# A graph network's front: one program ahead of the first edge pass, and the rest of the preparation beside it

## The chip, the cores and the metric

One core of one Trainium2 chip. The metric is the device time of one execution in microseconds; the kernel before was run three times. The profile is one execution of the same program, taken by the hardware profiler.

## What is computed

The inputs are 3125 nodes with 256 features, 50000 edges (src, dst, sorted by dst, and a weight), and the weights of four graph blocks. Each block is added to its input, and a layer norm follows:

```python
x = _layernorm(x + L0(x, src, dst, edge_weight, ...))   # 3 layers: linear, / sqrt(deg_out), per-channel product,
                                                        # weighted sum over the edges of a node, / sqrt(deg_in), relu
x = _layernorm(x + L1(x, src, dst, ...))                # max over edges of relu(theta(x_dst - x_src) + phi(x_src))
x = _layernorm(x + L2(x, edge_index, ...))              # attention with 8 heads, softmax over the edges of a node
x = _layernorm(x + L3(x, src, dst, ...))                # 3 layers: max over the edges of a *source*, batch norm, relu
```

So the kernel needs, beside the features: how many edges each node has as a source and as a target (deg_out, deg_in), where each node's edges begin and end in both orders, and for block L3 the order of the edges by source.

## The kernel before, in words

**Tiles.** 128 edges make a tile, 4 tiles a group: 392 tiles, 98 groups (`NG`). The nodes are 25 tiles. A program is a chain of stages (`Stage`), each with its own semaphores; every engine ends one stage before the next begins.

**Ahead of the first edge pass** (lines 261 to 716) come five stages, and then the node products n0:
- `constants`: identity, triangular masks, iotas.
- `edge_columns`: src, dst and weight are loaded, turned by TensorE and stored as columns; zeros are written to DRAM.
- `histogram(0)` counts by dst, with all weight loads beside it on SP. A node number is split into 98 high and 32 low digits. For 14 tiles at a time VectorE makes two one-hots (line 521, called from 550 and 551), TensorE multiplies them tile by tile (573), ScalarE copies the 98x32 counts of each tile to `HIST` (588). After 28 such steps VectorE adds `HIST` over the tiles (553) and forms starts by running sums (555 to 560), which go to DRAM.
- `histogram(1)` does the same by src. Beside it: the node numbers of dst (616 to 645), 25 indirect writes of marks by GpSimd (650), the weight transposes (387) and weight products (394, 400).
- `src_nodes`: 32 running sums over `HIST` (703), the numbers of src, and roots.
- `node_products("n0")`: per node tile a copy (1065), a transpose (993), a product (1000), ScalarE's scaled copy (1081) and VectorE's end (1086); each fifth tile SP stores five tiles of the table (1050). GpSimd writes the 25 marks of src.

**Edge passes** (`edge_pass`, 1096): e0, e1, e2 belong to the three layers of L0, e3 to L1, and others follow. Per group g: SP prefetches indices, mask and weights six groups ahead (1117 to 1120); GpSimd gathers four tiles (1146) into one of six sets; ScalarE scales them (1208, `scale`); TensorE turns them ("forth", 1161); VectorE runs a segmented scan in two halves (1191, `scan`); TensorE turns them back ("hither", 1170); ScalarE copies them (1215, `evac`); SP stores them. `pipelined` writes the order of each engine: every step has a lead, and step (fn, lead) does group s+lead in iteration s, in the order in which the steps are listed, "early" ones ahead of the pass's own and "late" ones behind.

**Rank work beside them** (`rank_beside`, 735): for each edge its place in the order by src. For one group of four tiles (a rank step k): one-hots on VectorE (521), "flip" on TensorE (787, 788), "take" on ScalarE (808 to 810), "meet" on TensorE (796 to 798), "places" on VectorE (769 to 776). "flip" k waits for "places" k-1, "places" k for "meet" k. Each of e0, e1 and e2 does a third of the steps, one every three groups. `order_beside` in e3 turns the ranks into the order.

Of the kernel before, what the change touches and what calls it, by code (L numbers as in the profile page):

```python
# [72 lines left out]
def pipelined(total, unroll, eng, *steps):  # L84

    most = max(lead for _, lead in steps)
    turns = (total - max(most, 3)) // unroll
# [8 lines left out]
    with eng.Fori(0, turns) as i:  # L98
        for j in range(unroll):
            for fn, lead in steps:  # L100
                fn(i * unroll + (j + lead), (j + lead) % unroll, i + (j + lead) // unroll)
    for s in range(turns * unroll, total):
        straight(s)
# [54 lines left out]
def build(nc, a, out):  # L158
    top = ExitStack()
    Stage.used = []  # L160
    with top:
# [7 lines left out]
        def carve(base, *wanted):  # L169
# [38 lines left out]
        HIST, key_hi, key_lo = carve(ARENA[:, NT * RW:NT * 3 * RW], ((ET, LO), F32), ((ET,), F32), ((ET,), F32))  # L208

        oh_hi, oh_lo, = carve(AGW_BASE, ((2, HB, HI), BF16), ((2, HB, LO), BF16))  # L210
        rank_hi, rank_lo, rank_t, rank_tf, rank_tmp, sel, rank = carve(
            AGW_BASE, ((2, RB, HI), BF16), ((2, RB, LO), BF16), ((2, 2, RB * P), BF16), ((2, RB * P), F32),
# [4 lines left out]
        key_tmp, iota_i, SRCF = carve(WORK, ((3, ET), I32), ((ET,), I32), ((ET,), F32))  # L217
# [12 lines left out]
        MW = sb("MW", [P, LAYERS, 2, D])  # L230
        TH1, DF1, W2 = sb("TH1", [P, 2, D]), sb("DF1", [P, 2, D]), sb("W2", [P, 2, D])
        WA = sb("WA", [P, 2, 2 * HEADS])
        TH3, DF3 = sb("TH3", [P, LAYERS, 2, D]), sb("DF3", [P, LAYERS, 2, D])
# [10 lines left out]
        MV = sb("MV", [P, NT, 2])  # L244
# [12 lines left out]
        flag_dst, flag_src = dram("flag_dst", [EP, 1]), dram("flag_src", [EP, 1])  # L257
        hist_start, hist_count = dram("hist_start", [2, NP]), dram("hist_count", [2, NP])


        def constants():
            with Stage(nc, "cst") as st:
                zeroed, filled, done = st.sem("zeroed"), st.sem("filled"), st.sem("done")
                copied = st.sem("copied")
                block = st.block()

                @block.gpsimd
                def _(eng):
                    eng.memset(ident[:, :], 0.0).then_inc(zeroed, 1)
                    eng.memset(ones[:, :], 1.0).then_inc(zeroed, 1)  # L270
                    eng.iota(iota_i[:, :], pattern=[[1, ET]], base=0, channel_multiplier=0).then_inc(zeroed, 1)
                    eng.wait_ge(zeroed, 3)
# [5 lines left out]
                    eng.affine_select(out=upto[:, :], in_=ones[:, :], compare_op=ALU.is_ge, fill=0.0,  # L278
                                      base=0, pattern=[[1, P]], channel_multiplier=-1).then_inc(filled, 1)

                @block.vector
                def _(eng):
                    eng.wait_ge(filled, 3)
                    eng.tensor_copy(identb[:, :], ident[:, :]).then_inc(copied, 1)
                    eng.tensor_copy(iota_b[:, :], iota_i[:, 0:P]).then_inc(copied, 1)
                    eng.tensor_copy(iota_h[:, :], iota_i[:, :]).then_inc(copied, 1)


        def weights_beside():


            fc, ch, mlp, th1, ph1, w2, fcb, fcb_wide, prod, AV = carve(
                WORK[:, 5 * ET:WORK.shape[1]], ((LAYERS * 2, D), F32), ((LAYERS * 2, D), F32), ((2, LAYERS * D), F32),
                ((2, D), F32), ((2, D), F32), ((2, D), F32), ((LAYERS * 2,), F32), ((LAYERS * 2, P), F32),
                ((2, 2, D), F32), ((2, D), F32))
            th3, ph3, B1b = carve(AGW_BASE[:, HB * (HI + LO):NT * RW], ((LAYERS * 2, D), F32), ((LAYERS * 2, D), F32), ((D,), F32))

            turns = [(lambda m, k, l=l: mlp[:, m, l * D + k * P:l * D + k * P + P], MW[:, l]) for l in range(LAYERS)]
            turns += [(lambda m, k: th1[:, m, k * P:k * P + P], TH1[:, :, :]),
                      (lambda m, k: ph1[:, m, k * P:k * P + P], DF1[:, :, :]),  # L300
                      (lambda m, k: w2[:, m, k * P:k * P + P], W2[:, :, :])]
            turns += [(lambda m, k, l=l: th3[:, 2 * l + m, k * P:k * P + P], TH3[:, l]) for l in range(LAYERS)]
            turns += [(lambda m, k, l=l: ph3[:, 2 * l + m, k * P:k * P + P], DF3[:, l]) for l in range(LAYERS)]
            banks = len(turns) + 2 * LAYERS

            def load_stage(st):
                loaded, zeroed = st.sem("loaded"), st.sem("zeroed")

                def on_sync(eng):
                    n = 0  # L310

                    def load(dst, src):
                        nonlocal n
                        eng.dma_start(dst, src).then_inc(loaded, 16)
                        n += 16

                    load(X[:, 0:NT - 1, :], a["x"][0:(NT - 1) * P, :].rearrange("(t p) d -> p t d", p=P))
                    eng.wait_ge(zeroed, 2)
                    load(X[0:LAST, NT - 1, :], a["x"][(NT - 1) * P:N, :])
                    load(fc, a["L0_gnn_fc_w"].rearrange("l (k p) i -> p (l k) i", p=P))  # L320
                    for c in range(4):
                        for l in range(LAYERS):
                            load(ch[64 * (c % 2):64 * (c % 2) + 64, 2 * l + c // 2, 64 * c:64 * c + 64],
                                 a["L0_gnn_ch_w"][l, c])
                    load(mlp, a["L0_gnn_mlp_w"].rearrange("(m p) i -> p m i", p=P))
                    with nc.allow_non_contiguous_dma("a bias across the partitions"):
                        load(fcb, a["L0_gnn_fc_b"].rearrange("l (k p) -> p (l k)", p=P))
                    for dst, name in ((th1, "L1_gnn_theta_w"), (ph1, "L1_gnn_phi_w"), (w2, "L2_gnn_W")):
                        load(dst, a[name].rearrange("(m p) i -> p m i", p=P))
                    for dst, name in ((th3, "L3_gnn_thetas"), (ph3, "L3_gnn_phis")):  # L330
                        load(dst, a[name].rearrange("l (m p) i -> p (l m) i", p=P))

                    def spread(dst, src, width):
                        load(dst, src.broadcast_to([P, width]))

                    spread(CHB[:, :, :].rearrange("p l d -> p (l d)"),
                           a["L0_gnn_ch_b"].rearrange("(o l) c d -> o (l c d)", o=1), LAYERS * D)
                    spread(MB[:, :], a["L0_gnn_mlp_b"].rearrange("(o d) -> o d", o=1), D)
                    spread(B1[:, :], a["L1_gnn_theta_b"].rearrange("(o d) -> o d", o=1), D)
                    spread(B1b, a["L1_gnn_phi_b"].rearrange("(o d) -> o d", o=1), D)  # L340
                    spread(AV[:, 0, :], a["L2_gnn_a_left"].rearrange("(o h) c -> o (h c)", o=1), D)
                    spread(AV[:, 1, :], a["L2_gnn_a_right"].rearrange("(o h) c -> o (h c)", o=1), D)
                    spread(GAM[:, :, :].rearrange("p l d -> p (l d)"),
                           a["L3_gnn_gammas"].rearrange("(o l) d -> o (l d)", o=1), LAYERS * D)
                    spread(BET[:, :, :].rearrange("p l d -> p (l d)"),
                           a["L3_gnn_betas"].rearrange("(o l) d -> o (l d)", o=1), LAYERS * D)
                    eng.wait_ge(loaded, n)

                def on_gpsimd(eng):
                    eng.memset(X[:, NT - 1, :], 0.0).then_inc(zeroed, 1)  # L350
                    eng.memset(ch, 0.0).then_inc(zeroed, 1)

                return dict(sync=on_sync, gpsimd=on_gpsimd)
# [1532 lines left out]
```

## Time and profile before

| what | us |
|---|---|
| median of three runs | 5416.98 |
| lowest, highest | 5415.43, 5417.36 |
| the profiled execution: span from first to last instruction (no other time of it is shown) | 5421.3 |
| busy in it: TensorE matmuls | 3436.3 |
| busy in it: VectorE | 3334.7 |
| busy in it: GpSimd | 3323.9 |
| busy in it: ScalarE | 1890.6 |

All times in rows are microseconds from the start of the span, unless marked ns. PE is TensorE's matmuls, PEld its weight loads, DVE VectorE, ACT ScalarE, POOL GpSimd, SP the engine that issues the other DMAs. "PEclk" is the granted clock of TensorE as a share of its full 2.4 GHz. L521 is line 521 of the kernel. The number in brackets at a row's end is the idle time of the engine in front of it, and what ended it. A line such as L521 belongs to a helper and stands for the calls in both counts and in the rank work.

### The profile page before, as it was taken

The page shows a single profiled execution, that of the slowest core. Times are in us where ns is not written, and L with a number is a line of the kernel's source. Part 1 is how long each engine was busy: PE and PEld are TensorE (multiplying, and loading weights), DVE is VectorE, ACT ScalarE, POOL GpSimd, SP SyncE. Part 2 cuts the span into 40 slices and gives each one's busy share as a digit, 9 for nine tenths or more (in the row PEclk, how much of TensorE's full clock was granted, in tenths as well). Part 3 has the DMA queues.
Part 4 walks back from the last instruction along what each step waited for, and adds up shares of the span by engine and source line. Part 5 has one row for each costly group of instructions (what it writes and reads, how often), then busy time and mean ns, then how long its engine had stood idle before and what let it go on. Part 6 is the DMA issues. An engine that isn't in the chain of part 4 may idle for free. (4 is left out here: it accounts for less than half of the span.)

```text
span 5421.3 us, 80197 instructions
## 1 busy us (share of the span) xinstructions
PE 3436.3 (63%) x18554; PEld 2760.3 (51%) x18554; DVE 3334.7 (62%) x6781; ACT 1890.6 (35%) x4275; POOL 3323.9 (61%) x3460
## 2 busy tenths in 40 slices
PE   3577777777787866666646664455556555665552
PEld 3456665666566655444534442355545555455451
DVE  8856655666566657999657775644444444444444
ACT  2256654666366643222223332222212222122221
POOL 1367765777477744777456664277752777357771
PEclk9778778788877778999666776777778777677776
DMA  3078875888488844888369995288853888358881
GB/s 89 16 197 235 235 210 151 239 234 234 128 236 234 235 136 137 234 233 234 110 170 241 248 242 152 65 230 236 237 163 103 236 237 236 96 169 235 236 230 52
DMA packets 965249, 1026.24 MB, mean 189 GB/s; under 512 B 312526, under 2 KB 843784, under 8 KB 965168
## 3 DMA queue, kind: packets, MB, share of 16 engines
q1 hardware_dynamic: 801184, 582.41, 36.8%
q0 software_dynamic: 163984, 442.92, 31.3%
q8 instruction: 30, 0.49, 0.0%
q14 instruction: 51, 0.42, 0.0%
HBM read 573.30 MB, written 449.41 MB: 189 GB/s over the span
## 5 line engine op out<-in xcount | busy, mean ns | idle before, releaser
L1146 POOL DMA_INDIRECT WORK<-table,idxbuf x2744 | 2609.6, 951 | 1319.6 <-issue 763.8
L1191 DVE TENSOR_TENSOR_SCAN WORK<-maskbuf,WORK,e_fm 128x512 f32<-128x512 bf16 x1372 | 1681.1, 1267 | 1293.7 <-PE e_fm L1161 1287.4
L1161 PE MATMUL e_fm<-ident,WORK 128*128 128x128 f32 x5488 | 997.2, 340 | 1044.1 <-DMA WORK<-table,idxbuf 717.5
L1161 PEld LDWEIGHTS e_fm<-ident,WORK 128*128 128x128 f32 x5488 | 790.1, 175 | 1218.8 <-DMA WORK<-table,idxbuf 725.2
L1215 ACT ACTIVATE WORK<-e_em 128x512 f32<-128x512 f32 x1372 | 757.1, 588 | 1607.6 <-PE e_em L1170 1491.3
L1170 PE MATMUL e_em<-ident,WORK 128*128 128x128 f32 x5488 | 995.2, 342 | 109.4 <-DVE WORK L1191 109.3
L1170 PEld LDWEIGHTS e_em<-ident,WORK 128*128 128x128 f32 x5488 | 884.6, 184 | 134.7 <-issue 112.4
L1208 ACT ACTIVATE WORK<-WORK,wbuf 128x256 f32<-128x256 f32 x1176 | 501.0, 496 | 605.2 <-DMA WORK<-table,idxbuf 605.2
L1545 POOL DMA_INDIRECT WORK<-table_attention,idxbuf x392 | 378.2, 965 | 189.5 <-issue 109.2
L1575 PE MATMUL att_o<-WORK 128*128 128x264 f32 x784 | 297.1, 543 | 0.0
L993 PE MATMUL n_t<-ident,WORK 128*128 128x128 f32 x450 | 108.9, 329 | 264.2 <-DVE WORK L966 156.3
L993 PEld LDWEIGHTS n_t<-ident,WORK 128*128 128x128 f32 x450 | 52.2, 156 | 339.0 <-DVE WORK L966 164.3
L1575 PEld LDWEIGHTS att_o<-WORK 128*128 128x128 f32 x784 | 199.5, 267 | 47.9
L521 DVE TENSOR_TENSOR ARENA<-ARENA,iota_b 128x128 bf16<-128x128 bf16 (+5 forms) x308 | 187.2, 665 | 1.4 <-DVEq L758 0.7
L1662 ACT ACTIVATE WORK<-att_o 128x264 f32<-128x264 f32 x392 | 151.1, 389 | 78.2 <-PE att_o L1575 73.4
L1559 PE MATMUL att_a<-ident,ARENA 128*32 128x128 f32 x98 | 33.4, 341 | 220.7 <-ACT ARENA L1649 220.1
L798 PE MATMUL e_ra<-ARENA 98*128 (+1 forms) x784 | 171.2, 302 | 0.0
L1329 PE MATMUL bn_ps<-ARENA,ones 128*128 128x256 f32 x300 | 105.0, 522 | 89.0 <-DVE ARENA L1355 79.0
L1559 PEld LDWEIGHTS att_a<-ident,ARENA 128*32 128x32 f32 x98 | 9.7, 99 | 274.9 <-ACT ARENA L1649 273.5
L798 PEld LDWEIGHTS e_ra<-ARENA 98*128 98x128 f32 x784 | 126.5, 203 | 28.8
L1329 PEld LDWEIGHTS bn_ps<-ARENA,ones 128*128 128x128 f32 x300 | 77.4, 266 | 116.6 <-DVE ARENA L1355 87.2
L844 DVE TENSOR_SCALAR ARENA<-iota_b,ARENA 128x128 bf16<-128x128 bf16 x392 | 133.3, 340 | 0.0
(282 smaller groups left out, 4519.9 us busy)
## 6 DMA issues: line engine op xcount, KB each, us to landing
edge_results<-WORK SPq DMA_DIRECT2D x686, 512.0 KB
edge_results_attention<-WORK SPq DMA_DIRECT2D x98, 544.0 KB
WORK<-table,idxbuf POOLq DMA_INDIRECT x2744
maskbuf<-nst_dst SPq DMA_DIRECT2D x294, 128.0 KB
maskbuf<-low_src SPq DMA_DIRECT2D x294, 128.0 KB, 4.9
ARENA<-dst_row SPq DMA_DIRECT2D x98, 256.0 KB
table<-ARENA SPq DMA_DIRECT2D x35, 640.0 KB, 3.2
maskbuf<-low_dst SPq DMA_DIRECT2D x98, 128.0 KB
```

Source lines behind the costliest of these rows:

```text
L521: return eng.tensor_tensor(dst, key[:, ds(t, n)].unsqueeze(2).broadcast_to([P, n, width]), iota_b[:, 0:width].unsqueeze(1).broadcast_to([P ...
L798: last = eng.matmul(pa[:, n * LO:(n + 1) * LO], rank_tf[0:HI, b, cols], HIST[0:HI, ds((k + first) * RB + n, 1), :].rearrange("p o l -> p ( ...
L993: last = eng.transpose(tp[slot][:, k * P:(k + 1) * P], R[:, slot, k * P:(k + 1) * P], ident[:, :])
L1146: eng.indirect_dma_start(G[:, q * GT + k, 0:D], None, T, bass.IndirectOffsetOnAxis(ap=idxbuf[:, q, k:k + 1], axis=0)).then_inc(got[q].sem, 16)
L1161: last = eng.transpose(fm[:, q % 2, h, k * P:(k + 1) * P], G[:, q * GT + k, h * P:(h + 1) * P], ident[:, :])
L1170: last = eng.transpose(em[:, pair, k, h * P:(h + 1) * P], S[:, q % 2, h, (2 * pair + k) * P:(2 * pair + k + 1) * P], ident[:, :])
L1191: last = eng.tensor_tensor_scan(S[:, q % 2, h, :], maskbuf[:, q, :], fm[:, q % 2, h, :], S[:, 1 - q % 2, h, GT * P - 1:GT * P], op0, op1)
L1208: last = eng.activation(G[:, q * GT + k, 0:D], G[:, q * GT + k, 0:D], ACT.Copy, scale=wbuf[:, q, k:k + 1])
L1215: eng.activation(O[:, q % 2, 2 * pair:2 * pair + 2, 0:D], em[:, pair], ACT.Copy).then_inc(pairs, 1)
L1329: last = eng.matmul(dst, ones[0:n, :], src[0:n, t, :], start=t == 0, stop=t == NT - 1)
L1545: eng.indirect_dma_start(G[:, q * GT + k, :], None, T2, bass.IndirectOffsetOnAxis(ap=idxbuf[:, q, k:k + 1], axis=0)).then_inc(got[q].sem, 16)
L1575: eng.matmul(po[:, k, 0:TW], same[:, q % 2, k, :], G[:, q * GT + k, :], start=True, stop=True).then_inc(made, 1)
```

## The change

- The stages from `constants` to n0 become one stage, `setup`. It loads src first, counts by src alone (28 steps, in two halves of 14, with the turning of dst and weight and the layer weight products of L0 between them), lets GpSimd add up `HIST` step by step, picks the counts of the nodes with one matmul, and makes the first table from X, whose turning reads X itself. The masks come from comparing each edge's dst with the edge before it; the marks of dst are gone.
- `e0` is written out flat (no loop) and carries in place of ranks: the count by dst (8 tiles a group, summed in PSUM), the node numbers of src and dst, the other weight loads and transposes, and the 32 running sums over `HIST`, one to a group.
- The ranks are done in e1 and e2, one step every two groups, with other leads and three buffers.
- The 25 marks of src move from n0 to n4. The keys of the one-hots become bf16.

```diff
-        HIST, key_hi, key_lo = carve(ARENA[:, NT * RW:NT * 3 * RW], ((ET, LO), F32), ((ET,), F32), ((ET,), F32))
+        HIST, key_hi, key_lo, dkey_hi, dkey_lo, node_f = carve(
+            ARENA[:, NT * RW:NT * 3 * RW], ((ET, LO), F32), *[((ET,), BF16)] * 4, ((6, NT), F32))
...
+                    eng.memset(added[0:HI], 0.0).then_inc(summed, 1)
+                    with eng.Fori(0, steps) as i:
+                        eng.wait_ge(held, i + 3)
+                        eng.wait_ge(summed, i + 1)
+                        eng.tensor_tensor(added[0:HI], added[0:HI], HIST[0:HI, ds(i * HB, HB), :], ALU.add).then_inc(summed, 1)
...
+                    split(SRCI[:, :], key_hi, key_lo)
...
+                    hots(0, half // 2)
+                    eng.wait_ge(gcn_in, 14 * 16)
+                    for q in range(2 * LAYERS):
+                        eng.tensor_scalar(fcb_wide[:, q, :], ones[:, :], fcb[:, q:q + 1], None, ALU.mult).then_inc(wide, 1)
+                    hots(half // 2 * 2, (steps - half // 2 * 2) // 2)
...
+                    eng.wait_ge(summed, steps + 1)
+                    c.link(eng.tensor_reduce(count_src[:, :], added[0:HI].rearrange("p t l -> p l t"), AX.X, ALU.add))
+                    c.link(spread_counts(c, count_src, spread[0:HI, :].rearrange("p (q l) -> p q l", q=4)))
+                    eng.sem_inc(spread_sem, 1)
+                    eng.wait_ge(picked, 1)
+                    c.link(eng.tensor_scalar(norm_out[:, :], picked_ps[:, 0:NT], 1.0, None, ALU.max))
...
+                def extras(g, q, turn):
+                    if g < groups:
+                        if g >= 2:
+                            eng.wait_ge(dmade, g - 1)
+                        one_hot(eng, dhi[:, g % 2], dkey_hi, g * DB, DB, HI).then_inc(dhot, 1)
+                        one_hot(eng, dlo[:, g % 2], dkey_lo, g * DB, DB, LO).then_inc(dhot, 1)
...
+                    if groups + 9 <= g < groups + 9 + LO:
+                        lo = g - (groups + 9)
                         c.inc(eng.tensor_tensor_scan(HIST[0:HI, :, lo], ones[0:HI, 0:1].broadcast_to([HI, ET]),
+                                                     HIST[0:HI, :, lo], start_src[:, lo:lo + 1], ALU.mult, ALU.add))
...
-        RANKS = -(-(ET // RB) // LAYERS)
+        RANKS = ET // RB // 2
-            first = layer * RANKS
-            steps = min(RANKS, ET // RB - first)
+            first = (layer - 1) * RANKS
+            steps = RANKS
...
-                        if q % 3 == phase and not (isinstance(g, int) and g // 3 >= steps):
-                            fn(turn * (SETS // 3) + q // 3, q // 3 % 2)
+                        if q % 2 == phase and not (isinstance(g, int) and g // 2 >= steps):
+                            fn(turn * (SETS // 2) + q // 2, q // 2)
...
-                    return [(at(0, meet), 0)], [(at(0, flip), 2)]
+                    return [], [(at(0, meet), 0), (at(0, flip), 1)]
...
-                    return [(at(0, take), 1)], []
+                    return [(at(0, take), 0)], []
...
-            node_products("n0", stage_copy(X), GW[:, 0], out1, None, out2, table=(AGG, T), marks=(first_src, flag_src))
             for l in range(LAYERS):
-                edge_pass(f"e{l}", SRCI, (ALU.mult, ALU.add), nst_dst, True, rank_beside(l))
+                edge_pass(f"e{l}", SRCI, (ALU.mult, ALU.add), nst_dst, True, rank_beside(l) if l else numbers_and_weights_beside)
...
-            node_products("n4", None, DF1, copy_to(AGG), TH1, out2, table=(AGG, T), norm=(add_bias,))
+            node_products("n4", None, DF1, copy_to(AGG), TH1, out2, table=(AGG, T), norm=(add_bias,), marks=(first_src, flag_src))
...
-        constants()
-        edge_columns()
-        load_weights, turn_weights = weights_beside()
-        histogram(0, DSTF, load_weights)
-        histogram(1, SRCF, both_beside(turn_weights, dst_nodes_beside))
-        src_nodes()
+        setup()
         flow_l0()
```

VectorE's steps of the rank work keep their leads: "places" early with lead 0 in odd groups, one-hots late with lead 3.

## Rows read from the trace of the kernel before

**Rows 1.** Windows: length, PE, PEld, DVE, ACT, POOL busy (count), PEclk, DMA share, GB/s
```profile
242.20:291.60 49.40, 37.33 (x158) 24.80 (x158) 18.70 (x53) 20.52 (x50) 24.48 (x25) 0.88 0.24 71
291.60:800.30 508.70, 390.48 (x2352) 326.80 (x2352) 313.77 (x623) 309.09 (x687) 374.39 (x392) 0.79 0.83 228
870.90:1380.00 509.10, 388.33 (x2360) 323.94 (x2360) 314.62 (x626) 308.13 (x686) 373.45 (x392) 0.79 0.81 227
...
2034.00:2090.00 56.00, 45.90 (x214) 34.74 (x213) 40.65 (x152) 29.45 (x81) 0.00 (x0) 1.00 0.14 50
```

**Rows 2.** Groups of instructions in e0 (291 to 785): busy and mean ns, idle before
```profile
L1146 POOL DMA_INDIRECT WORK<-table,idxbuf x392 | 374.4, 955 | 136.1 <-issue 106.0 <-DMA wbuf<-WE 30.1
```

**Rows 3.** Timeline (start, us): n0's last tile, e0's first and last gather
```profile
282.47 0.48 DVE L1086 SCALAR_TENSOR_TENSOR ARENA<-GB,norm_out,WORK 128x256 f32<-128x256 f32 x1 [0.38 <-ACT WORK L1081]
...
291.62 0.99 POOL L1146 DMA_INDIRECT WORK<-table,idxbuf  x1 [17.00 <-DMA wbuf<-WE]
...
784.19 0.94 POOL L1146 DMA_INDIRECT WORK<-table,idxbuf  x1 [0.30 <-issue]
```

**Rows 4.** Ahead of the first pass: groups by form, and the first count's timeline row
```profile
L521 DVE TENSOR_TENSOR ARENA<-ARENA,iota_b 128x1372 bf16<-128x1372 bf16 x56 | 88.6, 1583 | 0.7 <-DVE ARENA L512 0.7
L650 POOL DMA_INDIRECT flag_dst<-ones,first_dst x25 | 43.1, 1725 | 105.3 <-DVEq L673 97.9 <-issue 7.3
L553 DVE TENSOR_REDUCE count<-ARENA 98x32 f32<-98x12544 f32 x2 | 42.8, 21376 | 4.4 <-ACT ARENA L588 4.4
L521 DVE TENSOR_TENSOR ARENA<-ARENA,iota_b 128x448 bf16<-128x448 bf16 x56 | 34.8, 621 | 0.0
...
L703 DVE TENSOR_TENSOR_SCAN ARENA<-ones,startv,ARENA 98x392 f32<-98x392 f32 x32 | 29.7, 1009 | 5.2 <-PEq L155 5.2
...
20.13 57.02 DVE L521 TENSOR_TENSOR ARENA<-ARENA,iota_b 128x1372 bf16<-128x1372 bf16 x56 [0.35 <-DVE ARENA L512]
```

**Rows 5.** Timeline: the weight products of L0, the first and the last of them
```profile
183.64 1.89 PE L394 MATMUL w_ps<-WORK 128*128 128x256 f32 x8
...
191.62 0.38 ACT L416 ACTIVATE GB<-w_ps 128x256 f32<-128x256 f32 x1 [0.27 <-PE w_ps L400]
```

**Rows 6.** Timeline of TensorE in e2 at full clock: flip, forth (then hither), meet's first and last
```profile
1512.62 0.22 PE L787 MATMUL e_ra<-identb,ARENA 128*98 128x128 bf16 x1
...
1513.97 1.09 PE L1161 MATMUL e_fm<-ident,WORK 128*128 128x128 f32 x8
...
1515.77 0.22 PE L796 MATMUL e_rb<-ARENA 98*128 98x128 bf16 x1
...
1517.74 0.41 PE L798 MATMUL e_ra<-ARENA 98*128 x2
```

**Rows 7.** Timeline of ScalarE in e0: the first of take's three copies
```profile
784.73 0.58 ACT L808 ACTIVATE ARENA<-e_ra 98x512 bf16<-98x512 bf16 x1
```

**Rows 8.** Timeline of VectorE in e0: places, its first and last, and the scans
```profile
788.90 0.29 DVE L769 SCALAR_TENSOR_TENSOR ARENA<-e_rb,upto 128x128 bf16<-128x128 f32 x1 [1.40 <-PE e_ra L798]
...
790.39 0.16 DVE L776 TENSOR_TENSOR BYSRC<-ARENA 128x4 f32<-128x4 f32 x1
...
791.92 2.45 DVE L1191 TENSOR_TENSOR_SCAN WORK<-maskbuf,WORK,e_fm 128x512 f32<-128x512 bf16 x2 [1.37 <-PE e_fm L1161]
```

**Rows 9.** Timeline of TensorE in e2 at half clock: meet's first, then forth, hither
```profile
1531.18 0.31 PE L796 MATMUL e_rb<-ARENA 98*128 98x128 bf16 x1
...
1534.74 1.95 PE L1161 MATMUL e_fm<-ident,WORK 128*128 128x128 f32 x8
1536.48 1.91 PE L1170 MATMUL e_em<-ident,WORK 128*128 128x128 f32 x8
```

**Rows 10.** Windows (columns as in rows 1): a gap of TensorE in e2, and behind it
```profile
1549.90:1553.20 3.30, 0.38 (x4) 0.14 (x2) 2.61 (x3) 1.68 (x5) 2.43 (x3) 0.96 0.85 258
1553.20:1556.50 3.30, 3.22 (x16) 3.22 (x17) 1.03 (x1) 0.99 (x3) 2.65 (x3) 0.52 0.73 223
1556.50:1562.80 6.30, 5.18 (x40) 3.86 (x37) 4.23 (x5) 5.70 (x13) 4.78 (x6) 1.00 0.82 248
```

More of the change, by code:

```diff
@@ L97, in pipelined @@
         straight(s)
[L98 to L101, printed above, removed]
+    if turns:
+        with eng.Fori(0, turns) as i:
+            for j in range(unroll):
+                for fn, lead in steps:
+                    fn(i * unroll + (j + lead), (j + lead) % unroll, i + (j + lead) // unroll)
     for s in range(turns * unroll, total):
@@ new lines, in build, with one_hot @@
+        count_dst, start_dst, small = (v[0:HI] for v in carve(ROWSUMS, ((LO,), F32), ((LO,), F32), ((LO + 2,), F32)))
+        pick, rows_of = sb("pick", [HI, NT]), sb("rows_of", [HI, 4])
+        START, CNT, HAS, LASTE, T1, T2_ = range(6)
+        def one_hot(eng, dst, key, t, n, width):
+            return eng.tensor_tensor(dst, key[:, ds(t, n)].unsqueeze(2).broadcast_to([P, n, width]),
+                                     iota_b[:, 0:width].unsqueeze(1).broadcast_to([P, n, width]), ALU.is_equal)
@@ new lines, in _, with hots @@
+                    split(SRCI[:, :], key_hi, key_lo)
+                    def hots(first, turns):
+                        with eng.Fori(0, turns) as i:
+                            for b in range(2):
+                                n = i * 2 + (first + b)
+                                eng.wait_ge(made, n + 1)
+                                one_hot(eng, oh_hi[:, b], key_hi, n * HB, HB, HI).then_inc(hot_sem, 1)
+                                one_hot(eng, oh_lo[:, b], key_lo, n * HB, HB, LO).then_inc(hot_sem, 1)
@@ L602, in histogram @@
-            if which == 1:
-                gathered[0].close(NT)
-        node_f, flag_cols, mark_cols = carve(AGW_BASE[:, HB * (HI + LO) + (4 * LAYERS + 1) * D:NT * RW], ((6, NT), F32), ((ET,), F32), ((3, ET), BF16))
-        START, CNT, HAS, LASTE, T1, T2_ = range(6)
-        def load_numbers(eng, w, loaded):
-            with nc.allow_non_contiguous_dma("node numbers across the partitions"):
-                for k, h in ((START, hist_start), (CNT, hist_count)):
-                    eng.dma_start(node_f[:, k, :], h[w:w + 1, :].rearrange("o (t p) -> p (o t)", p=P)).then_inc(loaded, 16)
+                    eng.wait_ge(dst_in, 48)
@@ new lines, in _, with hold @@
+                    eng.activation(rows_f[:, 1], rows_i[:, 1], ACT.Copy).then_inc(cast_dst, 1)
+                    eng.sem_inc(held, 2)
+                    def hold(first, turns):
+                        with eng.Fori(0, turns) as i:
+                            for b in range(2):
+                                n = i * 2 + (first + b)
+                                eng.wait_ge(made, n + 3)
+                                eng.activation(HIST[0:HI, ds(n * HB, HB), :],
+                                               wide_ps[0:HI, b, 0:HB * LO].rearrange("p (k l) -> p k l", l=LO), ACT.Copy).then_inc(held, 1)
```

796 lines of the change are left out of this document (417 added, 379 removed).

## The prediction

> **What bounds the kernel now.** I read the stage table first. It cuts the run at the block borders: everything ahead of the first edge pass takes 291.6 us, of which the last 49.4 us are the first node products; then the edge passes e0 and e1 take 508.7 and 509.1 us each, with node products between them [rows 1]. The reader is to see two kinds of time. In an edge pass GpSimd holds the pace: 392 indirect gathers of 0.955 us busy, with 0.30 us of issue between two, so one every 1.25 us and 5.0 us for a group of four tiles; the last gather starts 492.6 us after the first, which is 391 times 1.26 [rows 2, 3]. In e1 VectorE is busy 315 of 509 us and TensorE 388, at a mean granted clock of 0.79 of full speed [rows 1]: both have room, but the rank work rides on that room. Ahead of the first pass, VectorE is the bound, with two counts in a row: 56 pairs of one-hots (1583 and 621 ns, a pair every 2.04 us, since 56 instructions take 57.0 us), two reductions of 21.4 us, and 32 running sums of 1.01 us [rows 4].
>
> **The part in front.** The change puts one program there. Its path, term by term:
> - Start of the count: today at 20.1 us [rows 4], behind three blocks and all nine edge loads. Now only src is awaited. I take 9 us, between 5 and 20.
> - 28 pairs for src alone: 57.0 us [rows 4], so 66.
> - TensorE leaves the count in the middle to turn two columns and to form the layer weights. The weight products took 8.0 us, 183.6 to 191.6 [rows 5], the turns perhaps 1.5; VectorE has six small products (1.3) and two one-hot pairs (4.1) in hand and waits for the rest. I add 7.5 us in all: 73.5.
> - Last matmuls, last copy and GpSimd's last addition: 3.5 us, so 77. GpSimd's addition of 98x448 has no row. Nothing, if it hides; if it takes 3 us where a step has 2.04, 28 steps cost 27 us more. I take it as hidden, nearest to VectorE's pair, which covers four times as many elements in 2.04 us.
> - The short reduction, the spreading, one matmul, root and reciprocal: 5 us, 82.
> - First node products without the copy ahead of each turn: they took 40.7 us (242.2 to 282.9) [rows 1, 3]; I take 36, so 118. Between its last tile and the first gather lay 8.7 us [rows 3], kept: first gather at 127.
>
> So the first gather moves from 291.6 to 127: **-165 us**, between -130 and -178. Gone are the second count's 57 us, both 21.4 us reductions, and the 32 sums from the path.
>
> **Work moved into e0.** Per group, VectorE's scans take 2.45 us [rows 8] and the new one-hots (1040 elements, against 1820 in 2.04 us [rows 4]) 1.2: 3.7 of 5.0 us. TensorE gets 8 small matmuls and, every second group, four turns. In return e0 loses its third of the ranks. The node numbers are bursts of a few us, and six sets of gathered tiles lie ahead. The weight loads, some 3.5 MB behind SP's prefetches, would be 15 us at the 228 GB/s of the pass [rows 1], and SP issues eight of them between the prefetches of groups 1 to 3. The 32 running sums come one to a group from group 58 on, 1.0 us in 2.5 free. I take **+3 us**, between 0 and +15; if the gathers' cover is gone, the prefetch is late next. The 25 marks for src go from n0 to n4, where GpSimd is idle for 56 us [rows 1]; at the dearest rate seen, 1.73+0.30 us each [rows 4], they need 51, and stand ahead of e3's gathers in GpSimd's queue. Nothing, and up to +5. The longer straight code of e0: nothing, bounded by the same +15.
>
> **The ranks, now in two passes instead of three.** This is what I think decides. The rank step runs every two groups (10.0 us of gathers) instead of every three (15.0), and its leads are shorter: TensorE's "meet" now stands behind hither(2k), and VectorE's "places" in front of scan(2k+1). Until now a whole iteration lay between them. Now they form a ring:
> - scan(2k) ends; hither(2k) 0.9; meet(k) 2.2 and its tail 0.3 (1515.8 to 1518.15) [rows 6]; places(k) 1.65 [rows 8]; scan(2k+1) 2.45 [rows 8];
> - then on VectorE one-hots 0.8 and scan(2k+2) 2.45, which closes the ring: 0.9+2.5+1.65+2.45+0.8+2.45 = 10.75, with waits some 10.85 us. On TensorE in the same time: hither 0.9, flip 1.35, forth 0.9, hither 0.9, meet 2.5 [rows 6] after the 4.1 of places and scan: 10.65. ScalarE's "take", three copies of 0.6 us that overlap to 1.5 [rows 7], fits beside forth and hither.
>
> So at full clock the ring already needs 10.85 us where gathers need 10.0. At half clock meet takes 3.55 and forth or hither 1.74 [rows 9]; flip I take as 1.8: 4.1+1.74+1.8+1.74+1.74+3.9 with waits is 15.4 us. TensorE stands still in each round from the end of forth(2k+2) to the end of scan(2k+1), about 3.5 us. The windows show what follows such a gap: after 3.3 us with 0.38 of work the clock of the next 3.3 us was 0.52, that is 1.2 GHz, and full (2.4 GHz) again behind it [rows 10]. If each round pays one such stretch, 3.3 us at half speed do 1.65 us of work and the round is 10.85+1.65 = **12.5 us**. A pass has 49 rounds: 49 x (12.5-10.0) = +122 us each, **+245** for e1 and e2, between 0 (the ring slips under the gathers after all) and +530 (15.4). What is queued behind: VectorE waits for "meet" with its scans behind it; TensorE's hither, ScalarE's copies, SP's stores and the next prefetches follow.
>
> **Sum.** The profiled execution shows its span alone, 5421.3 us, 4.3 above the median of 5417.0. 5421.3 - 165 + 3 + 245 = 5504; less 4.3: **5500 us**.
>
> **Rivals.**
> 1. Ring at full clock. TensorE has more work per us than before, which speaks for it; three passes at 0.79 [rows 1] speak against. Round 10.85: +42 per pass, 5339 us. Point of decision: the saved 162 us are 81 per pass, a round of 11.65 us. Below it the kernel is faster.
> 2. The gathers keep the pace, as in every pass now; e1 and e2 stay at 509: 5255. It needs an overlap that I don't see in the order of the code.
> 3. Half clock throughout: 15.4 a round, 5785. Against it: the clock came back in e1 each time.
> 4. GpSimd's addition paces the count (3 us a step): +27, 5527.
> 5. One-hots at twice the rate, since the keys are now bf16: 57 us become about 30, 5473. Against it: with f32 keys or bf16 keys there is no pair of rows to compare; today's pair runs at 1.1 ns an element [rows 4].
> 6. The program in front doesn't overlap as it says and the first gather comes at 200, 73 us later than I have it: 5573.
>
> On rival 5 the Trainium skill says both: "VectorE: DVE Perf Modes" gives the doubled rate to a two-source operation whose tensors are all 16-bit with step one; "Vector Engine (DVE) Microarchitecture Reference" (5.1, the triggers) adds that one element read again and again, as the key is here, ran at the single rate. By the first the sum would be 27 us less, by the second it stands.
>
> **How the numbers follow.** Forecast 0.48; rival 1 0.21; 2 0.13; 3 0.05; 4 0.04; 5 0.05; 6 0.04. A change under 0.2% (11 us) is about what a measurement of this kernel can't tell from none. Faster: rivals 1 and 2 and a tail of the forecast, 0.37; same 0.04; slower 0.59. The forecast's own range, rounds of 11.8 to 14.1 us, is 5430 to 5660. The range 5320 to 5650 takes in rival 1 with the bounds of the part in front and leaves out rivals 2 and 3, 0.18.
>
> **What would show it.** First gather near 127 us (the part in front). L521's mean in the count still about 1.58 us (rival 5). e0 still near 509 us. In e1 and e2: GpSimd's gathers wait for prefetched indices instead of issue, 392 gathers over some 600 us; VectorE's "places" group has a large idle time in front, released by TensorE's L798 line, near 3.4 us a round; granted clock 0.75 to 0.85. I am wrong in size if that clock is 1.0, and wrong in kind if gathers still follow each other every 1.25 us there, or if e0 or the marks in n4 have grown.

## Result, and the profile after

The changed kernel takes **5644.0 us** (median of 4, 5641.2 to 5658.6), the kernel before 5417.1 in the same comparison: a ratio of **1.0425**, 95% interval 1.041 to 1.044. So it is slower, as forecast, but by 227 us and not by 83, and it lies inside the given range by 6 us only. The profiled execution has a span of 5641.5 us; its ledger against the 5421.3 of before adds up to the difference of the two spans, 220 us. (The 227 us are those of the medians: the median lies 2.5 us above the profiled span here and lay 4.3 below it before.)

| stretch | before | after | difference | forecast |
|---|---|---|---|---|
| first gather of e0 | 291.6 | 139.9 | -151.7 | -165 |
| e0, first to last gather | 492.6 | 517.6 | +25.0 | +3 |
| e0's last gather to e1's first | 91.9 | 90.3 | -1.6 | 0 |
| e1, first to last gather | 491.6 | 650.8 | +159.2 | +122 |
| to e2's first gather | 91.1 | 108.6 | +17.5 | 0 |
| e2, first to last gather | 492.5 | 653.1 | +160.6 | +122 |
| to e3's first gather (n3, n4 and the marks) | 145.5 | 160.7 | +15.2 | 0 |
| all behind that | 3324.5 | 3320.5 | -4.0 | 0 |

The stages by windows, for [rows 1] (length, PE, PEld, DVE, ACT and POOL busy with their counts, PEclk, DMA share, GB/s): the part in front, e0, e1, e2, and e2's last tail with n3 and n4.

```profile
0.00:139.90 139.90, 78.57 (x592) 68.73 (x592) 100.92 (x112) 41.51 (x90) 48.21 (x53) 0.83 0.27 86
139.90:663.00 523.10, 309.08 (x1997) 287.58 (x1997) 341.08 (x384) 265.47 (x596) 393.72 (x392) 0.74 0.83 226
...
747.70:1420.00 672.30, 492.18 (x2723) 396.59 (x2723) 340.76 (x816) 336.18 (x733) 373.74 (x392) 0.74 0.62 171
...
1507.00:2182.00 675.00, 496.06 (x2729) 399.86 (x2729) 340.61 (x816) 336.60 (x733) 374.51 (x392) 0.74 0.61 170
2182.00:2320.90 138.90, 92.48 (x418) 67.40 (x417) 89.99 (x300) 55.33 (x152) 50.07 (x50) 0.88 0.18 57
```

In e1 GpSimd does the 373.7 us of work that it did before, over 672 us, and what the transfers move falls from 227 to 171 GB/s: neither sets the pace. In e0 the transfers keep 226 GB/s, but GpSimd is busy 393.7 us instead of 374.4 for the same 392 gathers.

**Who waits in e1.** The view of one line: the gathers of e1, then the first step of "places" there (count, shortest, median and longest duration in ns, first and last start; below it what its engine waited for).

```profile
L1198 POOL DMA_INDIRECT WORK<-table,idxbuf x392: 940/946/1304, 747.7 to 1398.6; - x196
its engine sat idle before it (us, times) until:
  DMA wbuf<-WE: 212.2, 53
  issue: 107.5, 339
...
L819 DVE SCALAR_TENSOR_TENSOR ARENA<-e_rb,upto x196: 284/286/293, 766.8 to 1422.7; 128x128 bf16<-128x128 f32 x196
...
  PE e_ra L848: 309.6, 49
```

The gathers wait for prefetched indices (212 us in 53 waits), and VectorE stands 309.6 us in 49 waits ahead of places, released by the last line of meet: 6.3 us a round. That is the forecast's signature with the wrong size, 3.4 us. From the first places to the first instruction of the last (1422.02 on the timeline) are 48 rounds in 655.2 us: **13.65 us a round**, where I had 12.5.

**One round**, on the timeline of e1 (start, length in us; a row can hold several instructions in a row):

```profile
1053.74 0.29 DVE L819 SCALAR_TENSOR_TENSOR ARENA<-e_rb,upto 128x128 bf16<-128x128 f32 x1 [6.35 <-PE e_ra L848]
...
1055.69 2.45 DVE L1243 TENSOR_TENSOR_SCAN WORK<-maskbuf,WORK,e_fm 128x512 f32<-128x512 bf16 x2 [0.17 <-issue]
...
1058.06 0.74 DVE L255 TENSOR_TENSOR ARENA<-ARENA,iota_b 128x392 bf16<-128x392 bf16 x2
...
1058.29 1.96 PE L1222 MATMUL e_em<-ident,WORK 128*128 128x128 f32 x8 [3.67 <-DVE WORK L1243]
1058.72 2.44 DVE L1243 TENSOR_TENSOR_SCAN WORK<-maskbuf,WORK,e_fm 128x512 f32<-128x512 bf16 x2
...
1060.04 0.31 PE L837 MATMUL e_ra<-identb,ARENA 128*98 128x128 bf16 x1
...
1061.99 1.97 PE L1213 MATMUL e_fm<-ident,WORK 128*128 128x128 f32 x8
...
1063.75 1.47 PE L1222 MATMUL e_em<-ident,WORK 128*128 128x128 f32 x8
...
1065.05 0.22 PE L846 MATMUL e_rb<-ARENA 98*128 98x128 bf16 x1
```

The order is the one that was read out of the code: places, scan(2k+1), then on TensorE hither (1058.3), flip (1060.0), forth (1062.0), hither (1063.8) and meet (1065.1), which releases the next places. TensorE stands 3.67 us for the scan, and comes back slowly: hither takes 1.96 us and forth 1.97, where forth took 1.09 at full clock [rows 6]. Windows over the same round, columns as above (the eleventh number is the granted clock):

```profile
1053.40:1058.20 4.80, 1.21 (x10) 0.98 (x10) 4.10 (x14) 0.60 (x2) 3.30 (x4) 0.96 0.64 195
1058.20:1064.00 5.80, 5.71 (x26) 4.65 (x27) 2.96 (x4) 3.10 (x7) 4.27 (x5) 0.50 0.60 180
1064.00:1067.60 3.60, 3.60 (x27) 2.94 (x26) 0.14 (x1) 3.60 (x10) 0.00 (x0) 0.91 0.66 126
```

Behind a window with 1.21 us of work in 4.8 the clock is 0.50 (1.2 GHz). It stays there for 5.8 us in which TensorE is busy 5.71, and for 0.6 us more: a window of 1064.0 to 1064.6 has 0.50 too, and one from there to 1067.6 has 1.00 (2.4 GHz). So TensorE does 6.3 us of its work slowly, from the start of hither until just before meet. From round to round this repeats: behind the first, the 47 rounds of e1 are all between 13.50 and 13.72 us long.

**The part in front.** Groups of VectorE and of GpSimd up to the first gather, by form (count, busy us and mean ns, idle before), for [rows 4]:

```profile
L255 DVE TENSOR_TENSOR WORK<-ARENA,iota_b 128x1372 bf16<-128x1372 bf16 x28 | 59.8, 2135 | 7.8 <-PE set_wide L417 7.4 <-DVE ARENA L486 0.4
L255 DVE TENSOR_TENSOR WORK<-ARENA,iota_b 128x448 bf16<-128x448 bf16 x28 | 20.2, 723 | 0.0
...
L334 POOL TENSOR_TENSOR WORK<-WORK,ARENA 98x448 f32<-98x448 f32 x28 | 39.9, 1424 | 49.3 <-ACT ARENA L552 48.7 <-POOL WORK L334 0.6
```

And the timeline: the start of the count, its short reduction, the last tile of the node products, the first gather, and four gathers of e0.

```profile
9.77 14.88 DVE L255 TENSOR_TENSOR WORK<-ARENA,iota_b 128x1372 bf16<-128x1372 bf16 x11 [0.35 <-DVE ARENA L486]
...
98.45 0.90 DVE L509 TENSOR_REDUCE count_src<-WORK 98x32 f32<-98x448 f32 x1 [3.05 <-POOL WORK L334]
...
130.89 0.48 DVE L528 SCALAR_TENSOR_TENSOR ARENA<-GB,norm_out,WORK 128x256 f32<-128x256 f32 x1 [0.60 <-ACT WORK L580]
...
139.88 1.11 POOL L1198 DMA_INDIRECT WORK<-table,idxbuf  x1 [41.53 <-DMA wbuf<-WE]
...
178.35 0.95 POOL L1198 DMA_INDIRECT WORK<-table,idxbuf  x1 [0.30 <-issue]
179.60 1.74 POOL L1198 DMA_INDIRECT WORK<-table,idxbuf  x1 [0.30 <-issue]
...
190.44 0.94 POOL L1198 DMA_INDIRECT WORK<-table,idxbuf  x1 [3.86 <-DMA wbuf<-WE]
...
197.40 0.94 POOL L1198 DMA_INDIRECT WORK<-table,idxbuf  x1 [2.09 <-DMA wbuf<-WE]
```

The same pair of one-hots that took 1583 and 621 ns before takes 2135 and 723 now: 18.3 us more over 28 pairs in busy time. GpSimd's addition is short, 1.42 us, and would fit beside a pair; but it doesn't run beside it for nothing. In e0 single gathers take up to 1.76 us instead of 0.945: 62 of the 392 rows of GpSimd's timeline are over 1.0 us (15 before), together 23 us over the rest, and VectorE is on a one-hot in 30.5 of those 81.7 us (of all 394 us of the gathers it is in 49). At 190.4 and 197.4 two gathers wait for prefetched indices: these are groups 9 and 10, whose prefetches are issued around the eight weight loads in SP's queue.

### The profile page after: what moved, and what is told of

The parts are those of the page before. It is cut to its first block and busy times, and to the rows that moved or that the text cites. A ratio compares the mean times of both kernels' runs of the same rounds, so it can differ in the third digit from the quotient of the medians.

```text
span 5641.5 us, 78233 instructions
## 1 busy us (share of the span) xinstructions
PE 3503.4 (62%) x18564; PEld 2828.2 (50%) x18564; DVE 3301.4 (59%) x6801; ACT 1869.6 (33%) x4237; POOL 3346.4 (59%) x3471
## 3 DMA queue, kind: packets, MB, share of 16 engines
q0 software_dynamic: 163184, 442.91, 30.5%
## 5 line engine op out<-in xcount | busy, mean ns | idle before, releaser
L1213 PE MATMUL e_fm<-ident,WORK 128*128 128x128 f32 x5488 | 1022.3, 347 | 1074.7 <-DMA WORK<-table,idxbuf 816.1
L1267 ACT ACTIVATE WORK<-e_em 128x512 f32<-128x512 f32 x1372 | 769.0, 590 | 2143.4 <-PE e_em L1222 2086.4
L1213 PEld LDWEIGHTS e_fm<-ident,WORK 128*128 128x128 f32 x5488 | 817.9, 180 | 1235.2 <-DMA WORK<-table,idxbuf 805.9
L1222 PE MATMUL e_em<-ident,WORK 128*128 128x128 f32 x5488 | 1054.9, 357 | 365.9 <-DVE WORK L1243 361.5
L1222 PEld LDWEIGHTS e_em<-ident,WORK 128*128 128x128 f32 x5488 | 933.9, 193 | 401.7 <-issue 357.8
L1595 POOL DMA_INDIRECT WORK<-table_attention,idxbuf x392 | 380.8, 971 | 186.9 <-issue 108.6
L819 DVE SCALAR_TENSOR_TENSOR ARENA<-e_rb,upto 128x128 bf16<-128x128 f32 x392 | 90.5, 287 | 622.1 <-PE e_ra L848 622.1
L1042 PE MATMUL n_t<-ident,WORK 128*128 128x128 f32 x400 | 97.1, 329 | 216.3 <-DVE WORK L1015 153.3
L1049 PE MATMUL n_m<-TURNED,WORK 128*128 128x256 f32 x600 | 180.0, 429 | 0.0
L1053 PE MATMUL n_m<-TURNED,WORK 128*128 128x256 f32 x600 | 158.8, 388 | 0.0
L255 DVE TENSOR_TENSOR ARENA<-ARENA,iota_b 128x392 bf16<-128x392 bf16 (+3 forms) x294 | 135.9, 504 | 0.5 <-DVEq L808 0.5
```

The lines of the kernel that those rows point to most:

```text
L1049: last = eng.matmul(mps[:, slot, 0:D], XT[:, slot, k * P:(k + 1) * P], w1[:, k, :], start=k == 0, stop=k == 1)
L1053: last = eng.matmul(mps[:, slot, D:D + n2], XT[:, slot, k * P:(k + 1) * P], w2[:, k, :], start=k == 0, stop=k == 1)
L1213: last = eng.transpose(fm[:, q % 2, h, k * P:(k + 1) * P], G[:, q * GT + k, h * P:(h + 1) * P], ident[:, :])
L1222: last = eng.transpose(em[:, pair, k, h * P:(h + 1) * P], S[:, q % 2, h, (2 * pair + k) * P:(2 * pair + k + 1) * P], ident[:, :])
L1267: eng.activation(O[:, q % 2, 2 * pair:2 * pair + 2, 0:D], em[:, pair], ACT.Copy).then_inc(pairs, 1)
L1595: eng.indirect_dma_start(G[:, q * GT + k, :], None, T2, bass.IndirectOffsetOnAxis(ap=idxbuf[:, q, k:k + 1], axis=0)).then_inc(got[q].sem, 16)
```

## The experiments

Four questions: is it the order of the rank step; is it the clock; what lengthens the one-hots; what lengthens e0. The lines are those of the changed kernel unless said otherwise. One thing has to be known to read the numbers: in the jobs whose labels have no number, and in that of both_2, two_hots_in_e0_2 and before_leads_moved_2, the transfers were slower, and the kernel before took 7167 to 7182 us instead of 5417. Windows over e0 in leads_restored, whose e0 is the changed kernel's, untouched:

```profile
138.00:807.00 669.00, 323.45 (x1992) 282.97 (x1993) 336.58 (x383) 267.92 (x591) 397.88 (x392) 0.66 0.62 176
```

176 GB/s where 226 were moved before. So the passes of those jobs say little about the order on the engines. The same kernels have further labels with a number, and the same expectations where none is quoted. The part in front can be read in either kind of job: the first gather came at 138.6 us in leads_restored and at 139.8 in leads_restored_2.

**1. The leads of the rank step restored.**

```diff
-                    return [], [(at(0, meet), 0), (at(0, flip), 1)]
+                    return [(at(0, meet), 0)], [(at(0, flip), 2)]
...
-                    return [(at(0, take), 0)], []
+                    return [(at(0, take), 1)], []
```

> Only the leads of the rank step change: TensorE's meet goes back ahead of forth (early), flip back to lead 2, ScalarE's take back to lead 1; the step stays at every second group. Theory ring (the order closes scan, hither, meet, places, scan into one chain of 13.3 us a round): the chain is open again, VectorE has 7.9 us of work in a round of 10, TensorE some 7.5 at full clock; e1 and e2 fall from 650.8 and 653.1 us (first to last gather) to between 492 and 520, and the time to about 5290 us. Rival period (a rank step every two groups is too much work for the pass in any order): at half clock forth, hither, flip and meet need 13.8 us a round, so the passes stay above 620 us and the time above 5580.

> The same kernel as leads_restored, since in the first job every transfer was slower than in the traces shown (the kernel before took 7169 us there, and e0, which the edit doesn't touch, 666 us from first to last gather instead of 518). Where the transfers run as in the trace of the changed kernel (e0 near 518 us), theory ring says e1 and e2 fall to between 492 and 520 us and the time to about 5290 us; rival period says passes above 620 us and a time above 5580.

With slow transfers: 6926 us, ratio 0.970 (0.961 to 0.979). There the restored order gains nothing in the passes: e1 and e2 take 747 and 738 us from first to last gather, and 728 and 717 in the same job with the changed kernel's order (the kernel of run 5). With normal ones: **5304.2 us** (4 runs) against 5419.1, ratio **0.979** (0.977 to 0.981). Windows of e1, and the view by line of the gathers and of places in e1:

```profile
747.70:1245.00 497.30, 440.36 (x2707) 356.40 (x2706) 343.64 (x816) 327.82 (x725) 373.75 (x392) 0.81 0.85 230
```

```profile
L1198 POOL DMA_INDIRECT WORK<-table,idxbuf x392: 940/946/1346, 750.2 to 1242.2; - x196
...
L819 DVE SCALAR_TENSOR_TENSOR ARENA<-e_rb,upto x196: 284/286/294, 764.8 to 1247.1; 128x128 bf16<-128x128 f32 x196
...
  PE e_ra L848: 53.5, 46
```

492 us from first to last gather, as in the kernel before, and VectorE waits 53.5 us for meet instead of 309.6, with the same work in the same 49 rounds, at the same period. Two leads and one place in TensorE's order are worth 340 us (5644.0 against 5304.2); which of the three does it alone wasn't tried. The rival of the period falls.

**2. The clock kept up in the order of the change.** TensorE makes 24 transposes of the unit matrix in front of every second hither, inside its pause; they compute nothing that is used.

```diff
+                        if "filler" in side and q % 2 == 1:
+                            eng.wait_ge(pairs, g * 2 + 3)
+                            for _ in range(side["filler"]):
+                                eng.transpose(em[:, 0, 0, 0:P], ident[:, :], ident[:, :])
                         eng.wait_ge(scanned, g + 3)
```

> The order of the changed kernel is kept, but ahead of every second hither TensorE makes 24 extra transposes of the unit matrix into a bank that is free then (about 2.7 us at full clock), inside the 3.9 us in which it now waits for the scan. Theory ring plus clock (the pause drops the granted clock to 0.50 and hither, flip and forth then take twice as long): the clock of e1 and e2 rises from 0.74 to above 0.95, a round falls from 13.3 us to about 10.9, each pass to some 530 us, the time to about 5395 us. Rival ring alone (the chain would be as long at full clock, for instance by semaphore waits): the round stays within 0.5 us of 13.3 and the time near 5640 or above.

> The same kernel as filler, for the same reason. Theory ring plus clock: granted clock of e1 and e2 above 0.95, a round of about 10.9 us, some 530 us a pass, near 5395 us in all. Rival ring alone: a round within 0.5 us of 13.3, near 5640 us or above. A third outcome, which the first job hints at (clock 0.74 in e1, GpSimd waiting 330 us for indices): the extra matmuls lengthen TensorE's own chain and the clock is not kept either, passes above 650 us.

With slow transfers 7041 us, with e1 and e2 at 790 and 836 us from first to last gather, above the 728 and 717 without the extra transposes; why isn't known. With normal ones **5388.3 us** (one run), 256 below the changed kernel, though TensorE has more to do. Windows of e1, and places:

```profile
747.70:1270.00 522.30, 468.29 (x3715) 398.47 (x3716) 328.62 (x789) 318.37 (x703) 366.07 (x386) 0.98 0.79 214
```

```profile
L819 DVE SCALAR_TENSOR_TENSOR ARENA<-e_rb,upto x196: 284/286/293, 771.9 to 1293.8; 128x128 bf16<-128x128 f32 x196
...
  PE e_ra L848: 175.5, 49
```

At a clock of 0.98 a round takes (1293.8 - 0.7 - 771.9)/48 = **10.86 us** (0.7 us from the first to the fourth instruction of places). The chain alone was forecast at 10.85. So of the 3.65 us by which a round passes the 10.0 of the gathers, 0.86 are the chain and 2.8 the clock. The "third outcome" (passes above 650 us) came only with slow transfers.

**3. The same leads in the kernel before**, at a step every three groups in three passes (lines of the kernel before).

```diff
-                    return [(at(0, meet), 0)], [(at(0, flip), 2)]
+                    return [], [(at(0, meet), 0), (at(0, flip), 1)]
...
-                    return [(at(0, take), 1)], []
+                    return [(at(0, take), 0)], []
```

> The kernel before, with its rank step every three groups in three passes, but with the leads of the changed kernel (meet late, flip lead 1, take lead 0). Theory ring: the chain is about as long as in the changed kernel, 13.3 us a round plus one scan more, against 15.0 us of gathers; at 2.45 us and a hither more it comes to between 15 and 16.5, so e0 to e2 grow from 492 to somewhere between 492 and 540 us and the time is 5417 to 5550. If the order alone did the damage whatever the period, each pass would grow by 159 us as in the changed kernel, to some 5890.

With slow transfers 7206 and 7225 us, beside 7167 and 7182 for the kernel before. With normal ones **5424.1 us** (one run) beside 5418.0: no difference that one run can tell. Windows of e1, the gathers of e1, and the waits there:

```profile
870.90:1380.00 509.10, 385.64 (x2337) 326.37 (x2337) 310.83 (x615) 315.34 (x684) 374.20 (x392) 0.74 0.81 227
```

```profile
L1146 POOL DMA_INDIRECT WORK<-table,idxbuf x392: 945/949/1316, 879.7 to 1372.2; - x196
```

```profile
DVE ARENA L769 <- PE e_ra L798: 121.0, 32, 5.3
```

The chain is there: VectorE now waits 121.0 us for meet in e1 (3.8 us each; 17.7 us in the kernel before), and the clock falls from 0.79 to 0.74. But 15 us of gathers a round cover it, 492.5 us as before. Behind the last gather of e0 and of e1 some 3 and 4 us are added. So the order alone costs at most a few us, the period alone (run 1) nothing from first to last gather, and both together 340 us.

**4. The ranks left out**, in e1 and e2 both (the passes behind then read other rows of the same size).

```diff
-... rank_beside(l) if l else numbers_and_weights_beside)
+... nothing_beside if l else numbers_and_weights_beside)
```

> Leaves out the whole rank work in e1 and e2 (the order by src that it feeds is replaced by the node numbers of src, so e5 to e7 read other rows of the same size). Whatever the mechanism inside the rank work, the two passes go back to the pace of the gathers: 492 us from first to last gather each, some 335 us less in all, near 5305 us. If e1 and e2 stay above 520 us, something other than the ranks (code, prefetches, edge loads) slows them, and both the ring and the period fall.

It ran with slow transfers only (6753 us), so the forecast of 492 us a pass stays untested; run 1 had answered the question. There e1 took 646.5 us from first to last gather, no more than the 667 of that run's e0, while with the ranks and restored leads it was 747 in the same job. So where transfers are slow, the ranks aren't free in the better order either.

**5. The total of the count by TensorE** instead of GpSimd's addition.

```diff
-                    with eng.Fori(0, steps) as i:
-                        ...
-                        eng.tensor_tensor(added[0:HI], added[0:HI], HIST[0:HI, ds(i * HB, HB), :], ALU.add).then_inc(summed, 1)
...
+                                    last = eng.matmul(total, oh_hi[:, b, k, :], oh_lo[:, b, k, :], start=False, stop=False)
```

> Leaves GpSimd's addition of the count out of the part in front; TensorE makes a second small matmul for each tile that accumulates the total in a bank of its own. Theory contention (VectorE's one-hots were 2135 and 723 ns there, 1583 and 621 before, because GpSimd's two-input addition runs beside them): they go back to near 1583 and 621 ns, the first gather moves from 139.9 to about 118 us, and the time falls by some 21 us, to 5620. Rival layout (the one-hots are slower because their buffers or keys lie elsewhere): they stay above 2050 ns and the first gather within 3 us of 139.9. If TensorE's doubled matmuls pace the count instead, the one-hots are short but a step takes over 2.1 us.

With slow transfers, which the part in front doesn't feel (6899 us in all): groups of VectorE up to 120 us, by form, and the first gather on the timeline:

```profile
L255 DVE TENSOR_TENSOR WORK<-ARENA,iota_b 128x1372 bf16<-128x1372 bf16 x28 | 44.5, 1588 | 17.6 <-PE set_pick L416 17.3 <-DVE ARENA L487 0.4
L255 DVE TENSOR_TENSOR WORK<-ARENA,iota_b 128x448 bf16<-128x448 bf16 x28 | 17.3, 619 | 0.0
```

```profile
130.43 1.11 POOL L1199 DMA_INDIRECT WORK<-table,idxbuf  x1 [121.55 <-DMA wbuf<-WE]
```

The one-hots are back at 1588 and 619 ns, so it was the addition beside them and not their layout. But the first gather moves by 9.5 us and not 21: VectorE now waits 17.3 us for the doubled matmuls instead of 7.4 for the pause alone. I had put the pacing by TensorE last.

**6. One-hots in two of e0's 49 groups only**, with the leads restored.

```diff
-                        one_hot(eng, dhi[:, g % 2], dkey_hi, g * DB, DB, HI).then_inc(dhot, 1)
-                        one_hot(eng, dlo[:, g % 2], dkey_lo, g * DB, DB, LO).then_inc(dhot, 1)
+                        if g < 2:
+                            ...
+                        else:
+                            eng.sem_inc(dhot, 2)
```

> Leads restored, and in e0 the one-hots for the count of dst are made in the first two of 49 groups only; the other groups count those two over again (the node numbers of dst, and so all sums over incoming edges, are other ones of the same size). Theory contention (62 gathers of e0 took over 1.0 us, 23 us more than the rest's 0.945 us in all, and VectorE was on the one-hots in 30.5 of those 81.7 us): e0 falls from 519 us to about 502, with fewer than 25 long gathers. Rival transfers (the weights' 2.4 MB more and the instruction loads of the straight code stretch e0): e0 stays above 512 us. TensorE's small matmuls are kept, so they aren't told apart from the rest.

With slow transfers e0 didn't fall. It took 687.6 and 688.5 us, 21 and 22 more than in the runs both and both_2 of the same jobs (666.2 and 666.4), for a reason that stays open, though the gathers over 1.0 us fell from 60 to 19 and from 57 to 22. With normal ones (the run two_hots_in_e0_3), the view by line and three rows of the timeline:

```profile
L1201 POOL DMA_INDIRECT WORK<-table,idxbuf x392: 942/946/2440, 140.2 to 648.2; - x196
```

```profile
182.40 0.94 POOL L1201 DMA_INDIRECT WORK<-table,idxbuf  x1 [2.19 <-DMA wbuf<-WE]
...
189.89 0.94 POOL L1201 DMA_INDIRECT WORK<-table,idxbuf  x1 [2.79 <-DMA wbuf<-WE]
...
197.22 0.94 POOL L1201 DMA_INDIRECT WORK<-table,idxbuf  x1 [2.65 <-DMA wbuf<-WE]
```

e0 takes 508.0 us instead of 519.3 (run 1) and 518.8 (run 7): the one-hots cost **about 11 us**, between the 17 of one theory and the less than 7 of the other. It is one run, and e0 with all its one-hots was 517.6 in the changed kernel and 523.3 in run 2, so 10 to 15 us fit. The rest is read in the same trace. Gathers wait for indices at groups 8 to 11, four waits of 8.4 us in all where 0.3 each is usual, so some 7 us near the weight loads; and 23 gathers are still over 1.0 us, by 9.7 us in all, with VectorE on the running sums (L737 there) in 10.3 of their 31.4 us. Both links, to the weight loads and to the running sums, are read and not tested.

**7. Both edits, 1 and 5.**

> The two edits together: the leads of the rank step restored, and the count's total accumulated by TensorE in place of GpSimd's addition. Theory ring gives 5304 (leads restored alone); theory contention takes off what the first gather moved in the run total_on_pe, 139.9 to 130.4 us, so 9.5 us: about 5294 us, under the kernel before by some 2.3%. If the earlier first gather is given back in e0 or later, it stays at 5304.

> The same kernel as both. Where the transfers run as in the traces shown: 9.5 us under leads_restored_2, so about 5294 us, 2.3% under the kernel before; if the earlier start is given back, 5304.

With slow transfers 6896 and 6928 us, ratios 0.963 (0.959 to 0.966) and 0.966 (0.962 to 0.970). With normal ones **5286.1 us** (5 runs) against 5418.0, ratio **0.9756** (0.9742 to 0.9769), and the view by line for e0:

```profile
L1199 POOL DMA_INDIRECT WORK<-table,idxbuf x392: 943/949/2007, 129.2 to 648.1; - x196
```

The first gather is 10.6 us earlier than in run 1 (139.8) and the span 11.4 us shorter (5284.4 against 5295.8): what the part in front gains arrives at the end. The medians of the two lie 18 us apart instead (5286.1 and 5304.2); the four runs of run 1 spread over 15.5 us, so the difference to the 9.5 forecast isn't one that they can tell. This version beats both kernels.

## Why the forecast was right in kind and short in size

The forecast was +83 us, the measured change +227. The 144 us between them are: 13.3 in the part in front, 22 in e0, 107.5 in e1 and e2 with what stands behind their last gathers, -5.6 in the other stretches, and 6.8 because the median lies above the profiled span and not below it.

- **Direction and mechanism: right, and shown.** The order of the code closes a chain hither, meet, places, scan, one-hots, scan. Undoing the order alone brings 340 us back; its length at full clock is 10.86 us, forecast 10.85.
- **The clock term is the step that failed: right in kind, mis-sized, and some 107 of the 144 us that were missing.** "If each round pays one such stretch, 3.3 us at half speed do 1.65 us of work ..." The stretch is 6.3 us of work at 0.50, of which half is 3.15 us; by run 2 it costs 2.8 us a round. The round is 13.65 and not 12.5. I took the length of the slow stretch from one gap, where the next window was back at full clock [rows 10]. The rows that I used for the prices at half clock said otherwise: meet begins slow at 1531.18, and hither, at 1536.48, is slow still [rows 9], over 7 us. A short and a long stretch were both in hand, and I priced with the shorter one. That a round pays 6.3 us and not 3.3 or 7 is measured; why it is that long stays open. Per pass 49 x 3.65 = 179 us, measured 177 and 176.
- **Where it shows: half right.** I set the whole loss inside the passes. The gathers run up to six groups ahead, so 159 and 161 us stand between first and last gather, and 17.5 and 15.2 behind the last one, while the chain works off what is gathered. With the -1.6 us between e0 and e1 that is all of the growth from e0's end to e3. The marks in n4 cost nothing that can be seen, as forecast: in run 1, where the chain is open, e2's last gather to e3's first takes 145.3 us with the marks, and took 145.5 before.
- **The part in front: -151.7, forecast -165.** Start at 9.8 (9 forecast); end of the count at 95.0 (73.5); reduction to reciprocal 7.5 us (8.5); node products 28.9 us (36); to the first gather 8.5 (8.7). The term that failed is "I take it as hidden": the addition's length is hidden, its effect on the one-hots isn't. Rival 4 had the right place and nearly the price (+27), with the wrong mechanism: GpSimd doesn't pace the count, it waits 48.7 us in it for ScalarE's copies. Node products 7 us cheaper than forecast made up a third.
- **e0: +25, forecast +3** and at most +15. I asked what VectorE had room for (3.7 of 5.0 us) and what the transfers added, and not what VectorE's work does to GpSimd, which sets the pace. Of it about 11 us are the one-hots (shown, by one run); some 5 to 7 stand near the weight loads (I had named 15 and then taken 3), and the rest goes with the running sums, both as read in the traces.
- **The other rivals.** Rival 1 (ring at full clock) is what run 2 made, 5388 with the other terms as they are; rival 2 (gathers keep pace) is run 1. Rival 3 had the clock low throughout; it was 0.74. Rival 5 is out: with bf16 keys and no addition beside it the one-hot takes 1588 ns (run 5), with the f32 keys of the kernel before it took 1583. (The "bf16" in a row is the type of one input alone; the rows of before don't show that of the keys.) Rival 6: the program in front does overlap.

On the addition the Trainium skill has the rule that I should have weighed. "SBUF — State Buffer", section "Who interferes with whom", says that a VectorE instruction with two inputs in SBUF contends with a GpSimd instruction that reads SBUF. The one-hot and the addition are such a pair, and 1583 against 2135 ns agrees. The same section takes it, as inferred, that such an instruction doesn't hold up GpSimd's making of descriptors; here the gathers went from 0.945 to as much as 1.76 us, and e0 lost some 11 us by the one-hots. The measurement decides; by what way a one-hot lengthens a gather no run here shows.

## What to carry to other kernels

When a step is put on a shorter period, follow it once around all engines: an order that was harmless at 15 us a round (run 3) and a period that was harmless in the old order (run 1) cost 340 us together, and the cure is the order, not less work. It is a cure only where the chain sets the pace: with slow transfers it gained nothing. Work on the critical chain right behind a pause of TensorE runs at half speed, so take the bounds of that price from the shortest and the longest slow stretch that the trace shows (3.3 and over 7 us before, 6.3 measured), and not from one of them. Before calling an idle engine's work free, look at which instructions of the bounding engine it runs beside: the addition on GpSimd slowed VectorE's one-hots, and VectorE's one-hots slowed GpSimd's gathers.

## What the hardware did that I had not expected

Extra matmuls made a program faster: 24 useless transposes a round in TensorE's pause (with normal transfers, one run) raised the granted clock of e1 from 0.74 to 0.98 and took the kernel from 5644 to 5388 us. A one-hot of 128x1372 took 35% longer, 2135 against 1583 ns, beside an addition on GpSimd that needs 1.42 us itself. And the transfers can be some 22% slower from one job to the next: e0 moved 176 GB/s and took 666 us from first to last gather, where the same code moved 226 GB/s and took 518. Each of the five jobs of the experiments had a chip of its own, three of them slow, so whether it was the chip isn't shown. The version of run 7 was there still 3.4 to 3.7% below the kernel before.
